# Row maxima of the first cross attention in row tiles, three banks at a time

## The reference

```python
# layer L0: x is 16 x 56 x 128, y is 16 x 1500 x 96, 16 heads of 8
x = layer_norm(x + mha(q, k, v) @ w_so + b_so, ln_g, ln_b)         # self attention
qc, kc, vc = x @ w_q + b_q, y @ w_k + b_k, y @ w_v + b_v
ca = mha(qc, kc, vc) @ w_co + b_co                                 # first cross attention
x = layer_norm(x + ca, ln_g, ln_b)
x = layer_norm(x + ff(x), ln_g, ln_b)
# layer L1: second cross attention, 16 heads of 64, same y
# inside mha: softmax(einsum('bhqd,bhkd->bhqk', qh, kh) / sqrt(8)) over 1500 keys, then times vh
```

## Time and profile before

| | |
|---|---|
| median of 3 runs | 1087.92 us (1087.25 to 1088.8) |
| the profiled execution | 1085.93 us, span 1084.1 us |
| busy in the span | PE 1009.3 us (93%), DVE 742.8 (69%), ACT 566.5 (52%), POOL 377.6 (35%) |
| first cross attention | 98.2 to 451 us, its prologue from 78.6 us |

### The profile page before, as it was taken

The page is one execution under the profiler, slowest core; times in us unless marked ns, Lnnn a source line. Parts: engine busy times, 40 slices in busy tenths (PEclk is TensorE's granted clock), DMA queues, the critical chain, the costliest instruction groups (busy, mean ns, idle before and its releaser), DMA issues. The chain is left out here.

```text
span 1084.1 us, 31631 instructions
## 1 busy us (share of the span) xinstructions
PE 1009.3 (93%) x12044; PEld 736.4 (68%) x12044; DVE 742.8 (69%) x1409; ACT 566.5 (52%) x1135; POOL 377.6 (35%) x273
## 2 busy tenths in 40 slices
PE   6847999999999999888779999999999999999997
PEld 3633677777777777646327777777777777777786
DVE  5748887788877887212786767767677677767752
ACT  3623777777767776532434444434454453444542
POOL 6512111211112113020106554545556444555542
PEclk9977999999999999979799999999999999999998
DMA  3514444434454332210020122111011211102100
GB/s 126 123 43 124 131 148 145 139 121 132 142 149 134 120 113 72 67 35 1 7 69 28 55 57 59 54 38 55 22 56 55 57 44 47 45 32 57 35 4 4
DMA packets 47021, 79.90 MB, mean 74 GB/s; under 512 B 6978, under 2 KB 33812, under 8 KB 46964
## 3 DMA queue, kind: packets, MB, share of 16 engines
q1 hardware_dynamic: 46964, 79.11, 24.8%
HBM read 50.93 MB, written 21.96 MB: 67 GB/s over the span
## 5 line engine op out<-in xcount | busy, mean ns | idle before, releaser
L1385 ACT ACTIVATE P<-PS 125x448 f32<-125x448 f32 x384 | 207.1, 544 | 265.0 <-PE PS L1294 263.1
L1275 POOL TENSOR_TENSOR Pl<-P 125x896 f16<-125x896 f32 x128 | 229.9, 1801 | 237.0 <-ACT P L1385 237.0
L1021 DVE TENSOR_REDUCE m<-PS 128x1 f32<-128x500 f32 x336 | 220.8, 675 | 114.8 <-PE PS L1012 112.9
L927 DVE TENSOR_REDUCE m_part<-PS 128x1 f32<-128x500 f32 x336 | 210.4, 673 | 60.4 <-PE PS L829 58.9
L1310 PE MATMUL PS<-cNh,P 125*128 125x97 f16 x1344 | 197.9, 208 | 0.1
L1312 PE MATMUL PS<-cNh,Pl 125*128 125x97 f16 x1344 | 197.4, 207 | 0.0
L1311 PE MATMUL PS<-cNl,P 125*128 125x96 f16 x1344 | 196.8, 206 | 0.0
L905 ACT ACTIVATE Pb<-PS 125x448 f32<-125x448 f32 x384 | 186.0, 547 | 19.7 <-PE PS L804 18.7
L1311 PEld LDWEIGHTS PS<-cNl,P 125*128 125x128 bf16 x1344 | 131.9, 98 | 25.4
L829 PE MATMUL PS<-KH,Qmx 128*128 128x500 f16 x336 | 129.5, 388 | 14.3 <-PEq L701 8.2
L1310 PEld LDWEIGHTS PS<-cNh,P 125*128 125x128 bf16 x1344 | 131.2, 98 | 15.7 <-issue 3.2
(11 more groups left out here) (167 smaller groups left out, 1484.3 us busy)
## 6 DMA issues: line engine op xcount, KB each, us to landing
Kst<-k_halves SPq DMA_DIRECT2D x144, 125.0 KB, 2.8
k_halves<-KH SPq DMA_DIRECT2D x16, 750.0 KB, 3.3
cx<-in_ctx SPq DMA_DIRECT2D x16, 562.5 KB
d_cx<-in_ctx SPq DMA_DIRECT2D x16, 562.5 KB
c_halves<-cHi SPq DMA_DIRECT2D x16, 281.2 KB, 2.7
c_halves<-cLo SPq DMA_DIRECT2D x16, 281.2 KB, 3.1
cTh<-c_halves SPq DMA_DIRECT2D x16, 281.2 KB, 3.1
cTl<-c_halves SPq DMA_DIRECT2D x16, 281.2 KB, 4.0
```

Of the source, the lines that this page charges most:

```text
L927: nc.vector.tensor_reduce(m_part[:, t, part:part + 1], PS[:, 6 + k % 2, 0:SP], AX.X, ALU.max).then_inc(s_reduced, 1)
L1021: nc.vector.tensor_reduce(m21[:, t, part:part + 1], PS[:, S1[k % 2], 0:SP], AX.X, ALU.max).then_inc(n_red, 1)
L1275: nc.gpsimd.tensor_tensor(Pl[:, c % NP], P1[:, c % NP], high, ALU.subtract).then_inc(n_low_p, 1)
L1385: nc.scalar.activation(P1[:, c % NP, half * HALF:(half + 1) * HALF], PS[0:KC, u % 3, 0:HALF], ACT.Exp).then_inc(n_exp, 1)
```

## The change

The 896 rows of a batch are cut into 8 tiles of 112 rows instead of 7 of 128. The 128 partitions of `Qmx` and `KH` are four groups of 32, with four heads (224 rows) each; a tile is half of a group's rows and takes only the group's 32 partitions, so it is a matmul with 32 contraction rows (a 32x128 tile of the array) instead of 128. Three tiles (three entries e of the list of three key parts by four groups, with the same j, the half of the group's rows) make one `score_three`, into banks 5, 6 and 7; one `reduce_three` takes the maximum of all three at once. There are 8 triples a batch in place of 21 pieces; their places are c = 0, 3, 6, 9 right behind the chunk's scores (EARLY) and c = 1, 4, 7, 10 at the chunk's end (LATE). Triple k waits for the reduction of triple k-1. The scores have banks 0 and 1, and half u waits for exponential u-2. The prepared work moves from banks 5 and 3 to 2 and 3, the turned maxima from bank 7 to 5. The maxima's rows in Kst and Qst become 16 instead of 14, with a mask of their own in the table (C_MT). The second cross attention keeps its 21 pieces under the name NPC1.

```diff
-        OB, WB, WB2, MB = 4, 5, 3, 7
+        OB, WB, WB2, SB0, MB = 4, 2, 3, 5, 5
-        PIECES = [(t, part) for part in range(NSP) for t in range(QT)]
-        NPC = len(PIECES)
-        BESIDE = [range(min(2 * c, NPC), min(2 * c + 2, NPC)) for c in range(NC + LAG0)]
+        NPC = 2 * NSP * G // 3
+        EARLY = {0: 0, 3: 2, 6: 4, 9: 6}
+        LATE = {1: 1, 4: 3, 7: 5, 10: 7}
+        def three(k):
+            return k % 2, range(3 * (k // 2), 3 * (k // 2) + 3)
...
-                        wait_for(pe, exp_done, n * 2 * NC + u - 2)
+                        wait_for(pe, exp_done, n * 2 * NC + u - 1)
...
-                            mm = pe.matmul(PS[0:KC, u % 3, (g % 2) * 224:(g % 2 + 1) * 224],
+                            mm = pe.matmul(PS[0:KC, u % 2, (g % 2) * 224:(g % 2 + 1) * 224],
...
-                def score_piece(i, par, k):
+                def score_three(i, par, k):
                     slot, n = (par + 1) % 2, i * 2 + par + 1
-                    t, part = PIECES[k]
+                    j, where = three(k)
                     if k == 0:
                         pe.wait_ge(qmx_laid, n + 1)
-                    if t == 0:
-                        pe.wait_ge(k_high, n * 3 + part + 1)
-                    wait_for(pe, s_reduced, n * NPC + k - 1)
-                    pe.matmul(PS[:, 6 + k % 2, 0:SP], Qmx[:, slot, t * 128:(t + 1) * 128],
-                              KH[:, slot, 0, part * SP:(part + 1) * SP], start=True, stop=True).then_inc(s_filled, 1)
+                    if j == 0:
+                        pe.wait_ge(k_high, n * 3 + where[-1] // G + 1)
+                    wait_for(pe, s_reduced, n * NPC + k)
+                    for at, e in enumerate(where):
+                        part, g = e // G, e % G
+                        rows_of = slice(32 * g, 32 * g + 32)
+                        mm = pe.matmul(PS[0:TP, SB0 + at, 0:SP], Qmx[rows_of, slot, (2 * g + j) * TP:(2 * g + j + 1) * TP],
+                                       KH[rows_of, slot, 0, part * SP:(part + 1) * SP], start=True, stop=True)
+                    mm.then_inc(s_filled, 1)
...
-                def reduce_piece(i, par, k):
+                def reduce_three(i, par, k):
...
-                    nc.vector.tensor_reduce(m_part[:, t, part:part + 1], PS[:, 6 + k % 2, 0:SP], AX.X, ALU.max).then_inc(s_reduced, 1)
+                    j, where = three(k)
+                    nc.vector.tensor_reduce(m_part[:, where[0]:where[-1] + 1, j], PS[0:TP, SB0:SB0 + 3, 0:SP], AX.X, ALU.max).then_inc(s_reduced, 1)
...
-                        pieces = list(BESIDE[c]) if has_1 else []
-                        for k in pieces[:1]:
-                            score_piece(i, par, k)
+                        if has_1 and c in EARLY:
+                            score_three(i, par, EARLY[c])
...
-                        for k in pieces[1:]:
-                            score_piece(i, par, k)
+                        if has_1 and c in LATE:
+                            score_three(i, par, LATE[c])
```

More of the change, by code:

```diff
@@ L57 @@
 MR = 2 * QT
+QT0 = NQ // TP
+MR0 = 2 * QT0
 ON = 100
@@ L61 @@
 TWO_ONES = float(np.array(0x3C003C00, np.uint32).view(np.float32))
-C_ID, C_M4, C_MM, C_M16, C_MV, C_M8, C_END = 0, 128, 132, 139, 155, 157, 165
+C_ID, C_M4, C_MM, C_M16, C_MV, C_M8, C_MT, C_END = 0, 128, 132, 139, 155, 157, 165, 173
 def shape_table():
@@ L75, in shape_table @@
     t[:, C_MV:C_M8] = r // SQ == np.arange(2)
-    t[:, C_M8:C_END] = r % 64 // DH0 == np.arange(8)
+    t[:, C_M8:C_MT] = r % 64 // DH0 == np.arange(8)
+    t[:, C_MT:C_END] = (r >= 96) * (r < 96 + MR0) * ((r - 96) % QT0 == np.arange(QT0))
     return t
@@ L166, in program @@
         KH = sb_in(cross, "KH", [D, 2, 2, SK], F16)
-        Kst = sb_in(cross, "Kst", [96 + MR, 2, G, SK], F16)
+        Kst = sb_in(cross, "Kst", [96 + MR0, 2, G, SK], F16)
         Vst = sb_in(cross, "Vst", [KC, 2, NC, PAIRS, 32])
[L169 to L172, removed]
+        m_part = sb_in(cross, "m_part", [TP, NSP * G, 2])
+        mtop = sb_in(cross, "mtop", [TP, QT0])
+        mhigh = sb_in(cross, "mhigh", [TP, QT0], F16)
+        mneg = sb_in(cross, "mneg", [TP, MR0])
         Os = sb_in(cross, "Os", [128, 5 * SQ])
@@ L354, in lay_own_keys @@
             nc.gpsimd.tensor_tensor(Kbd[:, slot, j], SKT[:, bass.ds(t * 2 + j, 1), :].broadcast_to([D, H // 2, SQ]),
-                                    spread(tab[:, C_M8:C_END], 2, SQ), ALU.mult).then_inc(s_kbd, 1)
+                                    spread(tab[:, C_M8:C_MT], 2, SQ), ALU.mult).then_inc(s_kbd, 1)
         table_in, x_in, qkv_in, bqk_in, bv_in, wkv_in, later_in = (
@@ L382, in _ @@
                 pool.wait_ge(ones_set, 1)
-                nc.gpsimd.memset(Kst[96:96 + MR].bitcast(F32), TWO_ONES).then_inc(ones_set, 1)
+                nc.gpsimd.memset(Kst[96:96 + MR0].bitcast(F32), TWO_ONES).then_inc(ones_set, 1)
                 pool.wait_ge(ones_set, 2)
@@ L619, in program @@
         beyond = ExitStack()
-        Qst = sb_in(beyond, "Qst", [96 + MR, 2, G, GH * SQ], F16)
+        Qst = sb_in(beyond, "Qst", [96 + MR0, 2, G, GH * SQ], F16)
         Qmx = sb_in(beyond, "Qmx", [D, 2, NQ], F16)
@@ L847, in turn_maximum @@
                     pe.wait_ge(m_ready, n + 1)
-                    pe.matmul(PS[96:96 + MR, MB, 0:128], mneg[:], ident, start=True, stop=True).then_inc(m_turned, 1)
+                    pe.matmul(PS[96:96 + MR0, MB, 0:TP], mneg[:], ident[0:TP, 0:TP], start=True, stop=True).then_inc(m_turned, 1)
                 def body(i, par):
@@ L944, in body @@
                     for c in range(NC):
-                        pieces = list(BESIDE[c]) if has_1 else []
-                        for k in pieces[:1]:
-                            reduce_piece(i, par, k)
+                        if has_1 and c in EARLY:
+                            reduce_three(i, par, EARLY[c])
                         if has_2 and not at_start and 1 <= c < 4:
@@ L953, in body @@
                             normalise(b - 1)
-                        for k in pieces[1:]:
-                            reduce_piece(i, par, k)
+                        if has_1 and c in LATE:
+                            reduce_three(i, par, LATE[c])
                     if has_1:
@@ L958, in body @@
                         dve.wait_ge(s_reduced, n * NPC + NPC)
-                        nc.vector.tensor_reduce(mtop[:], m_part[:], AX.X, ALU.max).then_inc(m_link, 1)
+                        nc.vector.tensor_reduce(mtop[:].rearrange("p (g j) -> p g j", j=2), m_part[:].rearrange("p (s g) j -> p g j s", s=NSP), AX.X, ALU.max).then_inc(m_link, 1)
                         dve.wait_ge(m_link, n * 2 + 1)
@@ L963, in body @@
                         wait_for(dve, m_turned, n)
-                        nc.vector.tensor_scalar(mneg[:, 0:QT], mhigh[:], -1.0, None, ALU.mult)
-                        nc.vector.tensor_tensor(mneg[:, QT:], mhigh[:], mtop[:], ALU.subtract).then_inc(m_ready, 1)
+                        nc.vector.tensor_scalar(mneg[:, 0:QT0], mhigh[:], -1.0, None, ALU.mult)
+                        nc.vector.tensor_tensor(mneg[:, QT0:], mhigh[:], mtop[:], ALU.subtract).then_inc(m_ready, 1)
                         dve.wait_ge(m_turned, n + 1)
-                        nc.vector.tensor_tensor(Qst[96:96 + MR, slot].rearrange("p g c -> p (g c)").rearrange("p (t q) -> p t q", t=QT),
-                                                spread(PS[96:96 + MR, MB, 0:128], 1, QT),
-                                                spread(tab[96:96 + MR, C_MM:C_M16], 2, 128), ALU.mult).then_inc(m_laid, 1)
+                        nc.vector.tensor_tensor(Qst[96:96 + MR0, slot].rearrange("p g c -> p (g c)").rearrange("p (t q) -> p t q", t=QT0),
+                                                spread(PS[96:96 + MR0, MB, 0:TP], 1, QT0),
+                                                spread(tab[96:96 + MR0, C_MT:C_END], 2, TP), ALU.mult).then_inc(m_laid, 1)
                 over_pairs(dve, body, before=((-1, 1),))
@@ L990, in program @@
         PIECES1 = [(t, part) for part in range(NSP) for t in range(QT)]
+        NPC1 = len(PIECES1)
         def load_halves(sp, i, par, half, queries_made=None, ahead=False):
@@ L1048, in pieces_beside @@
         def pieces_beside(n):
-            return range(min(2 * max(n - H - 4, 0), NPC), min(2 * max(n - H - 3, 0), NPC))
+            return range(min(2 * max(n - H - 4, 0), NPC1), min(2 * max(n - H - 3, 0), NPC1))
         with nc.Block() as block:
@@ L1218, in program @@
         Z = sb_in(late, "Z", [TP, D])
-        BESIDE1 = [range(NPC * min(max(c - 1, 0), 9) // 9, NPC * min(c, 9) // 9) for c in range(NC + LAG)]
+        BESIDE1 = [range(NPC1 * min(max(c - 1, 0), 9) // 9, NPC1 * min(c, 9) // 9) for c in range(NC + LAG)]
         n_cn, n_cnl = sem("n_cn"), sem("n_cnl")
```

3 lines of the change are left out of this document (1 added, 2 removed).

## The result

| | before | after |
|---|---|---|
| median | 1088.36 us (1087.25 to 1090.06) | 1137.04 us (1135.16 to 1137.57) |
| ratio to before | | 1.0439, interval 1.0419 to 1.0458 |
| profiled execution, its span | 1085.93, 1084.1 us | 1137.54, 1135.7 us |
| 13 batches, 1 to 13, mean of one | 22.63 us | 25.30 us |

The account below looks back on a forecast made before the run. PE was taken as the bound, with slack on DVE and ACT. Batches 0 to 13 (34.0), batch 14 (2.2), batch 15 (2.3) and prologue (3.0) add 41.5 us: median 1129 us, range 1111 to 1145, 8 in 10 for 1103 to 1152.

Parts of the forecast that it names:

- the likeliest case: First cross attention: waits between DVE and PE outlast what PE saves, 1129 us; chance 0.82, part of it beyond a bound.
- prologue: Stretch from 78.8 to 98.1 us: eight triples of 1.72 us with fills between them end about 3.0 us later.
- batches 0 to 13: Full batches of the first cross attention: 24.77 us against 22.34 in the walk, 2.43 us more each, 34.0 us.
- batch 15 to the first score of the second cross attention: Last batch, only the two-bank score loop: a pair of chunks takes 2.67 us instead of 2.28, 2.3 us over six pairs.
- the hand-overs: Between DVE and PE at each triple: 0.06 us from DVE to PE, 0.47 from first tile's start to DVE's start.
- the walk: One batch stepped through the engines' in-order instructions: 24.77 us changed, 22.34 for before (measured 22.63), so 0.3 us short.
- the two loops: Within a batch: reductions alone, with three score banks, 24.77 us; two-bank scores waiting for exponentials, reductions free, 23.1 us.
- rival 1: First cross attention: PE's saving shows, waits sink into slack, 1.9 us less a batch, about 1061 us; chance 0.07.
- Rival 3: Row tiles do not run side by side: a triple holds PE 0.66 us, 27.86 us a batch, 1176 us; chance 0.08.
- PE is the bound: First cross attention before the change: PE has about 21.5 us of own work in a 22.6 us batch; DVE and ACT have some slack.
- PE's busy share lower with the clock still at its upper level: Expected sign in the changed kernel's profile, as in batch 15: 12.83 us busy of 14.00, clock share 1.00.
- a cold fill: Prologue, clock share taken as 0.67: filling a triple between two reductions takes 0.62 us, uncovered except by three splits.

## Why the prediction came true, and what was mis-sized in it

The forecast was 1129 us, the result 1137.04, inside the forecast's own range; the likeliest case was the one that came. The sum, term by term, against the two profiled executions (us):

| term | forecast | measured | from |
|---|---|---|---|
| start of the first piece or triple | 0 | +2.64 | 78.81, 81.45 |
| prologue, from there to the first score | +3.0 | +3.97 | 19.47, 23.44 |
| batches 0 to 13 | +34.0 | +37.08 | 318.48, 355.56 |
| batch 14 | +2.15 | +4.61 | 20.15, 24.76 |
| batch 15 to the first score of the second cross attention | +2.34 | +3.10 | 129.58, 132.68 |
| the rest | 0 | +0.21 | 517.65, 517.86 |
| sum | +41.5 | +51.6 | spans 1084.14, 1135.75 |

**The mechanism was right, and nearly each of its terms.** The reduction takes 1.720 us (forecast 1.72), the hand-overs 0.05 and 0.47 us (0.06 and 0.47). Three tiles last 0.42 us together where one has 0.413, so all three start within 0.007 us (0.0035 apart, where 0.007 was taken), and a triple holds PE 0.35 us with the change of shape behind it (0.273 and 0.09). Against the walk, in us from the batch's first score: triple 1 at 2.85 (forecast 2.73), triple 2 at 5.19 (4.99), triple 3 at 8.76 (8.58), the next batch at 25.03 (24.77, and 0.3 by which the walk was known to be short). Alone, the two loops were to give 24.77 and 23.1 us; with the other loop short they gave 25.15 and 23.43. PE's waits were to be some 4 us a batch: the seven brackets of PE in that batch add up to 2.59 us, with 0.17 for each 3.8, and waits too short for a bracket are not in it. The difference of 2.43 us a batch became 2.5 where nothing disturbs it: of batches 1 to 13 without batch 5 the mean is 25.17 us.

**PE's saving (rival 1) did not show, as argued.** That it is there follows from prices alone, 0.35 us for a triple of tiles, and 0.09 for the shape change ahead of most, against 0.64 for three full pieces; the 21.60 us a batch with both loops short does not tell it from waits that went. The reason put against it held: the reduction with its 1,500 columns does not end before PE is back. The Trainium skill's page "TensorEngine Tiling (Array Packing)", section "PSUM Bottleneck", which says that tiling speeds up TensorE and not the emptying of PSUM, agrees in that a reduction of a third of the columns gave 1.9 us a batch back; but with all 1,500 columns and another order it was 3.4 us, so the columns cost what the order lets them cost. **Rival 3 fell:** tiles of 32 rows run side by side, and with full pieces in their place a batch takes 1.3 us more (1.5 between batches that no fall of the clock touches, 26.52 and 25.03).

**"PE is the bound" was not the whole of it.** The prediction set 21.5 us of PE's own work against 22.6 and took the rest for granted; reordered, the kernel before runs at 21.26, so order set part of its batch too. It did not matter to the sum, which is a difference of two walks over the orders as they stand.

**What failed is the step "PE's busy share lower with the clock still at its upper level".** It was read from batch 15 and does not hold throughout. These are three stretches of after, one behind the other:

```profile
130.00:249.80 119.80, 106.86 (x1547) 70.60 (x1546) 93.30 (x104) 80.10 (x169) 18.78 (x25) 1.00 0.39 122
249.80:253.20 3.40, 3.40 (x44) 2.37 (x45) 1.81 (x2) 1.01 (x2) 0.00 (x0) 0.50 0.61 153
253.20:464.80 211.60, 187.54 (x2741) 123.64 (x2739) 162.21 (x184) 139.78 (x293) 34.69 (x46) 1.00 0.39 117
```

Within batch 5, after 120 us in which PE was busy 89%, the granted clock is 0.50 (1.2 GHz) for 3.4 us; that batch takes 26.83 us where batches 7, 9 and 11 take 25.3 to 25.4: 1.5 us. In batch 14 it is 0.51 for 6.9 us (464.80 to 471.70, above). Batch 14 prepares no later context, so the kernel with the splits first has the same order there as after; in its profile the clock stays up:

```profile
445.98:468.48 22.50, 19.21 (x311) 12.95 (x307) 15.96 (x16) 13.80 (x29) 8.74 (x7) 1.00 0.01 2
```

22.50 us against 24.76: 2.26 us of batch 14's excess of 2.46 is the clock; by the forecast, 20.15 and 2.15, it would have been 22.30. The clock fell once more in batch 15, for 3.4 us from 488.73. The stretch, then ACT's first exponentials of batch 15 in after, and the same in the kernel before with two score banks, where the clock stayed up:

```profile
488.73:492.15 3.42, 3.23 (x38) 2.27 (x38) 0.00 (x0) 1.59 (x4) 0.00 (x0) 0.50 0.00 0
...
485.65 4.33 ACT L915 ACTIVATE Pb<-PS 125x448 f32<-125x448 f32 x8
491.65 2.02 ACT L915 ACTIVATE Pb<-PS 125x448 f32<-125x448 f32 x4 [1.68 <-PE PS L811]
...
451.91 4.09 ACT L905 ACTIVATE Pb<-PS 125x448 f32<-125x448 f32 x8
456.70 2.02 ACT L905 ACTIVATE Pb<-PS 125x448 f32<-125x448 f32 x4 [0.69 <-PE PS L804]
```

From the first exponential to the ninth it is 6.00 us in after and 4.79 without the fall: 1.2 us. The three places together are 5.0 us, half of the 10.1 by which the sum is short; the prologue has another 1.0, and the 2.6 ahead of it are not the change's (both below).

**The prologue was mis-sized by 1 us.** The clock was 0.50 in all of it, not 0.67 as before. Between two reductions the trace has:

```profile
82.16 1.72 DVE L937 TENSOR_REDUCE m_part<-PS 112x3 f32<-112x1500 f32 x1 [6.24 <-PE PS L839]
84.66 1.72 DVE L937 TENSOR_REDUCE m_part<-PS 112x3 f32<-112x1500 f32 x1 [0.77 <-PE PS L839]
87.23 1.72 DVE L937 TENSOR_REDUCE m_part<-PS 112x3 f32<-112x1500 f32 x1 [0.86 <-PE PS L839]
```

DVE waits 0.77 to 0.86 us for a fill, not the 0.62 that I took for a cold fill; before, seven reductions stood nearly back to back at that place. How much of it is the clock is not shown: no run has this prologue at the upper level. **The 2.64 us ahead of the first triple are not the change's:** kernels whose instructions are those of before up to that place start their first piece at 79.96 us (the kernel before with two score banks) and 82.98 us (the kernel before reordered), against 78.81 in the profile shown. **Batch 15** has 2.71 us a pair of chunks where 2.67 was forecast (ScalarE's sets of four start at 491.65 and 494.36); without the fall of the clock it costs 2.24 us to its last exponential (15.39 in the kernel before with two score banks, 13.15 before), 2.34 forecast. So the term was right, and the 3.10 of the table are 2.24, the clock's 1.2 and 0.35 less behind the batch, which is not resolved.

**What stays open:** why the clock fell in batches 5, 14 and 15 and not elsewhere. PE's busy share alone does not tell. With full pieces three at a time, 150 to 400 us and batch 14:

```profile
150.00:400.00 250.00, 220.04 (x3080) 150.31 (x3079) 166.22 (x197) 156.33 (x329) 36.46 (x50) 1.00 0.39 117
477.47:502.50 25.03, 21.88 (x308) 14.46 (x304) 14.24 (x15) 13.90 (x29) 8.74 (x7) 0.93 0.01 2
```

PE was busy 88% in the first stretch and the granted clock was 1.00 throughout; in batch 14, at 87%, it fell to 0.50 for 3.4 us, and again in batch 15. The run with the exponential short had a fall in batch 14 too (24.58 us), those with the reduction short did not (20.55 and 18.99); the run with the splits first had none up to batch 14, but 6.8 us in batch 15 and 3.4 behind that. Whether it falls in the same places in every execution of after is not known. The Trainium skill, "TensorE: Matmul & The Clock Gate", section "A second HAM failure mode: psum-queue depth-cycling", tells of a kernel in which short idles between groups of matmuls, as it goes round the banks, make the clock change to and fro; that there are falls at all in after and with full pieces agrees with it, but batches 6 to 13 of both kernels have the same idles and no fall, so it does not tell when they come.

## What to carry to other kernels

Two engines that hand a buffer back and forth with one set of banks pay for the whole turn, fill and reading, plus everything that stands between them in each engine's order; so an engine that saves work at the price of a second buffer can lose, even if every engine has slack by amount. The price depends on the order: with triples filled while DVE splits, the same instructions took 21.86 us a batch instead of 25.30. Before such a change, walk one period step by step over the in-order queues with measured durations: that walk, with its constant 0.3 us, gave the period of eight of the nine changed kernels here to within 0.25 us (of the ninth, with both loops short, to 0.4). And a TensorE that the profile shows 97% busy can still give back 6% of a batch to a better order, since the modelled ends of matmuls hide part of its waits: look at the order before the amount of work. The order alone took the kernel before to 1069 us; the change, with its order written anew as well, came to 1086.

## What the runs showed of the hardware that was not expected

- The granted clock fell to its lower level inside a stage in which PE was busy 89%: 3.4 us in batch 5, 6.9 us in batch 14 and 3.4 us in batch 15, at a cost of 1.5, 2.3 and 1.2 us. Before, with PE busy 97%, the same stage had none from 103 us to the end of batch 15.
- A reduction out of three banks costs its columns and one fixed part and nothing for the banks: 1.720 us for 1,500 columns and, in the run with short reductions, 0.682 us for 504 out of the same three banks, which is 1.04 ns a column and 0.16 us; 500 columns of one bank take 0.673.
